# An LSTM step on one Trainium2 core: the scaled output gate is made on ScalarE instead of VectorE

## The chip, the cores and the metric

The kernel runs on one NeuronCore of a Trainium2 chip. TensorE (PE in the profile) multiplies matrices, VectorE (DVE) and ScalarE (ACT) work on tiles of up to 128 partitions, GpSimd (POOL) only clears some tiles at the start, and SyncE (SP) issues DMAs. Each engine takes its own instructions in order; engines wait for one another through semaphores. The metric is the time of one execution in microseconds (us), lower is better. Before the change the median of three runs is 1932.01 us (1931.52 to 1932.36).

## The reference

An LSTM with 512 hidden features runs over 512 time steps for a batch of 16, with float32 inputs, and its hidden states are added to the input:

```python
def step(carry, xw_t):
    prev_h, prev_c = carry
    a = xw_t + prev_h @ Wh
    i = sigmoid(a[:, :H]); f = sigmoid(a[:, H:2*H]); o = sigmoid(a[:, 2*H:3*H])
    g = tanh(a[:, 3*H:])
    next_c = f * prev_c + i * g
    next_h = o * tanh(next_c)
    return (next_h, next_c), next_h
# xW = x @ Wx + b for all steps;  output = x + hs
```

Step t+1 needs the h of step t, so 512 passes of the same chain stand one behind the other.

## The kernel before, in words

**The matmuls.** Every float32 factor is split into a high and a low float16 part, after scaling by a power of two. The weights stay in SBUF in both parts, with 256 columns to a matmul. One step is 128 matmuls of 32 columns of stationary data by 256 moving columns: 64 for the input part of the *next* step (`input_part`, L261), 32 with the low part of Wh (`recurrent_low`, L267) and 32 with the high part (`recurrent_high`, L273). The result lies in a PSUM tile `acc[par][n]`, where `par` is the parity of the step and `n` (0 or 1) one of two groups of 256 hidden features. ScalarE writes the bias into the tile ahead of the matmuls (`place_bias`, L202).

**The step behind the matmuls.** For each group n:

1. VectorE transposes the tile (`turn`, L439) and adds the two halves to the preactivations (`add_all` L448 for group 0; `add_three` L443 and `add_last` L451 for group 1).
2. ScalarE takes the tanh of three gates at once (`three_gates`, L216) and of the output gate alone (`last_gate`, L222). A sigmoid is made from a tanh of half the argument: sigmoid = (tanh + 1) / 2.
3. VectorE makes the two products of the cell (`gate_products`, L456) and the new cell (`new_cell`, L466); ScalarE takes the tanh of the cell (`tanh_of_cell`, L227).
4. The output gate is brought to (tanh + 1) times a scale of one number per partition, `scales[following][:, 1:2]` (`output_gate`, L461). It reads the tile of `last_gate`.
5. VectorE multiplies gate and cell tanh to the high half of h (`high_of_h`, L472), once more to the full h (`full_h`, L476), and subtracts to get the low half (`low_of_h`, L481).

**What the semaphores say.** TensorE waits for `h_high_ready` (counted by `high_of_h`) before the low-weight matmuls and for `h_ready` (counted by `low_of_h`) before the high-weight ones. It takes, in order: 16 low-weight matmuls on group 0 of h; 8 high-weight ones once the low half of h of group 0 is there; 8 low-weight ones once the high half of group 1 is there; then 8 high-weight ones once the low half of group 1 is there, which end `acc[par][0]` and let `turn(0)` start; 24 more end `acc[par][1]`; then come the 64 of the next step's input. `high_of_h(n)` waits for `h_parts_ready[n]`, which `output_gate(n)` and `tanh_of_cell(n)` count up by one each.

**The order** of all this is written out by hand, in the functions' calls at the end of each engine's step loop; no scheduler moves anything. The 512 steps come in 32 chunks of 16. Besides the above some steps carry work for the next chunk: input halves (ScalarE L183, VectorE L422), a search for the largest input (VectorE L517), one matmul L314 in step 8 of a chunk, and the scale of the next chunk in steps 9 to 13.

Of the kernel before, what the change touches and what calls it, by code (L numbers as in the profile page):

```python
# [5 lines left out]
ALU = mybir.AluOpType  # L6
ACT = mybir.ActivationFunctionType
# [8 lines left out]
NG = 2  # L16
CHUNK = 16
# [6 lines left out]
def lstm_kernel(nc, x, h0, wx, wh, bias, out):  # L24
# [7 lines left out]
    with ExitStack() as ctx:  # L32
        def sb(name, shape, dt):
            return ctx.enter_context(nc.sbuf_tensor(name, shape, dt))
# [4 lines left out]
        def sem(name):  # L39
            return ctx.enter_context(nc.semaphore(name))  # L40
# [29 lines left out]
        scales = [sb(f"scales{i}", [128, 4], F32) for i in range(2)]  # L70
# [10 lines left out]
        gates = [[sb(f"gates{p}{n}", [128, 5, 2 * B], F32) for n in range(NG)] for p in range(2)]  # L81
        products = [sb(f"products{n}", [128, 2, 2 * B], F32) for n in range(NG)]
        o_gate = [sb(f"o_gate{n}", [128, 2 * B], F32) for n in range(NG)]
# [38 lines left out]
        o_ready = sem("o_ready")  # L122
        products_ready = sem("products_ready")
        cell_ready = sem("cell_ready")
        h_parts_ready = [sem(f"h_parts_ready{n}") for n in range(NG)]
# [7 lines left out]
        @block.sync  # L133
        def _(sp):
            for c in range(C):
                sp.dma_start(w32["wx"][:, c, 0:Q], wx[:, c, 0:Q]).then_inc(w_loaded["wx"][c], 16)
            sp.dma_start(x_ring[0][:], x[:, 0:CHUNK, :]).then_inc(x_loaded[0], 16)
            for c in range(C):
                sp.dma_start(w32["wh"][:, c, 0:Q], wh[:, c, 0:Q]).then_inc(w_loaded["wh"][c], 16)
            sp.dma_start(x_ring[1][:], x[:, CHUNK:2 * CHUNK, :]).then_inc(x_loaded[1], 16)  # L140

            for first in range(0, T, QUARTER):
                chunk, at = divmod(first, CHUNK)
                half, slot = divmod(at, HALF)
                sp.wait_ge(out_ready, first + QUARTER)
                sp.dma_start(out[:, first:first + QUARTER, :], out_ring[half][:, slot:slot + QUARTER]).then_inc(out_free[half], 16)
                if chunk + 2 < CHUNKS:
                    sp.dma_start(x_ring[chunk % 2][:, at:at + QUARTER], x[:, first + 2 * CHUNK:first + 2 * CHUNK + QUARTER, :])\
                        .then_inc(x_loaded[chunk % 2], 16)
            for half in range(2):  # L150
                sp.wait_ge(out_free[half], 32 * CHUNKS + 1)
# [12 lines left out]
        @block.scalar  # L164
        def _(act):
            for c in range(C):
                act.dma_start(w32["wx"][:, c, Q:], wx[:, c, Q:]).then_inc(w_loaded["wx"][c], 16)
            act.dma_start(h0_feat[:], h0).then_inc(h0_loaded, 16)
            for c in range(C):
                act.dma_start(w32["wh"][:, c, Q:], wh[:, c, Q:]).then_inc(w_loaded["wh"][c], 16)  # L170
            act.dma_start(b_rows[:], bias).then_inc(b_loaded, 16)

            def high_of_w(k, n, c, done):
                act.activation(w_high[k][:, c, :, 0:64], w32[k][:, c, :, 0:64], ACT.Copy, scale=scale_bits[:, n:n + 1].bitcast(F32))
                act.activation(w_high[k][:, c, :, 64:GL], w32[k][:, c, :, 64:GL], ACT.Copy, scale=half_scale[:, n:n + 1])\
                    .then_inc(done, 1)

            act.wait_ge(wx_scale_ready, 1)
            for c in range(C):
                high_of_w("wx", 0, c, wx_high_done)  # L180
            def high_of_x(chunk, q):
                steps = slice(QUARTER * q, QUARTER * q + QUARTER)
                act.activation(x_halves[:, steps, :, 0, :], x_ring[chunk % 2][:, steps, :].rearrange("p t (c b) -> p t c b", b=B),  # L183
                               ACT.Copy, scale=scales[chunk % 2][:, 0:1]).then_inc(x_high_ready, 1)

            rescale = [act.alloc_register(f"rescale{p}") for p in range(2)]
            b_scale = [act.alloc_register(f"b_scale{p}") for p in range(2)]
            act.wait_ge(wh_scale_ready, 1)
            high_of_w("wh", 1, 0, wh_high_done)
            act.wait_ge(x_loaded[0], 16)  # L190
            act.wait_ge(x_scale_ready, 1)
            high_of_x(0, 0)
            high_of_w("wh", 1, 1, wh_high_done)
            high_of_x(0, 1)
            high_of_w("wh", 1, 2, wh_high_done)
            high_of_w("wh", 1, 3, wh_high_done)
            act.reg_load(rescale[0], inverses[0][0:1, 3:4])
            act.reg_load(b_scale[0], scales[0][0:1, 3:4].bitcast(I32))

            def place_bias(t):  # L200
                for n in range(NG):
                    act.activation(acc[t % 2][n][:, 0:GL], b_rows[:, n], ACT.Copy, scale=b_scale[t // CHUNK % 2])\  # L202
                        .then_inc(bias_placed, 1)

            act.wait_ge(b_ready, 1)
            act.wait_ge(acc_opened, 2 * NG)
            place_bias(0)

            for t in range(T):
                par = t % 2  # L210
                chunk, at = divmod(t, CHUNK)
                if t + 1 < T:
                    place_bias(t + 1)
                def three_gates(n):
                    act.wait_ge(preact_ready, NG * t + n + 1)
                    act.activation(gates[par][n][:, 1:4, :], preact[n][:, 0:6].rearrange("p (g c) b -> p g (c b)", c=2), ACT.Tanh,  # L216
                                   scale=rescale[chunk % 2]).then_inc(gates_ready, 1)

                def last_gate(n):
                    if n == 1:  # L220
                        act.wait_ge(o_preact_ready, t + 1)
                    act.activation(gates[par][n][:, 4, :], preact[n][:, 6:8].rearrange("p c b -> p (c b)"), ACT.Tanh,  # L222
                                   scale=rescale[chunk % 2]).then_inc(o_ready, 1)

                def tanh_of_cell(n):
                    act.wait_ge(cell_ready, NG * t + n + 1)
                    act.activation(cell_tanh[n][:], gates[1 - par][n][:, 0, :], ACT.Tanh, scale=0.5)\  # L227
                        .then_inc(h_parts_ready[n], 1)

                three_gates(0)  # L230
                last_gate(0)
                three_gates(1)
                tanh_of_cell(0)
                last_gate(1)
                tanh_of_cell(1)
                if at in (0, 1):
                    high_of_x(chunk, at + 2)
                if at in (13, 14) and chunk + 1 < CHUNKS:
                    if at == 13:
                        act.wait_ge(x_loaded[(chunk + 1) % 2], 16 + 16 * QUARTERS * ((chunk + 1) // 2))  # L240
                        act.wait_ge(x_scale_ready, chunk + 2)
                    high_of_x(chunk + 1, at - 13)
                    if at == 14:
                        act.reg_load(rescale[(chunk + 1) % 2], inverses[(chunk + 1) % 2][0:1, 3:4])
                        act.reg_load(b_scale[(chunk + 1) % 2], scales[(chunk + 1) % 2][0:1, 3:4].bitcast(I32))
# [71 lines left out]
        def _(dve):  # L317
# [112 lines left out]
            for t in range(T):  # L430
                par = t % 2
                chunk, at = divmod(t, CHUNK)
                later = (chunk + 1) % 2
                following = (t + 1) // CHUNK % 2
                nth = [NG * t + n + 1 for n in range(NG)]
# [14 lines left out]
                def add_last(n):  # L450
                    dve.tensor_tensor(preact[n][:, 6:8], turned[n][:, 6:8, 0, :], turned[n][:, 6:8, 1, :], ALU.add)\  # L451
                        .then_inc(o_preact_ready, 1)
# [3 lines left out]
                    dve.scalar_tensor_tensor(products[n][:], gates[par][n][:, 2:4, :], 1.0, gates[par][n][:, 0:2, :],  # L456
                                             ALU.add, ALU.mult).then_inc(products_ready, 1)

                def output_gate(n):
                    dve.wait_ge(o_ready, nth[n])  # L460
                    dve.tensor_scalar(o_gate[n][:], gates[par][n][:, 4, :], 1.0, scales[following][:, 1:2], ALU.add, ALU.mult)\  # L461
                        .then_inc(h_parts_ready[n], 1)

                def new_cell(n):
                    dve.wait_ge(products_ready, nth[n])
                    dve.scalar_tensor_tensor(gates[1 - par][n][:, 0, :], products[n][:, 0, :], 0.5, products[n][:, 1, :],  # L466
                                             ALU.mult, ALU.add).then_inc(cell_ready, 1)
# [19 lines left out]
                gate_products(0)  # L487
                add_three(1)
                new_cell(0)
                output_gate(0)  # L490
                add_last(1)
                gate_products(1)
                high_of_h(0)
                new_cell(1)
                full_h(0)
                output_gate(1)
                low_of_h(0)
                high_of_h(1)
                full_h(1)
# [81 lines left out]
```

## Time and profile before

| what | value |
|---|---|
| median of the runs | 1932.01 us |
| profiled execution, its own time | 1936.5 us |
| its span, first to last instruction | 1934.7 us |
| granted TensorE clock, share of full speed | 0.998 |
| PE busy | 1877.5 us, 97% of the span |
| DVE busy | 1816.8 us, 94% |
| ACT busy | 990.9 us, 51% |
| output gate on DVE (L461) | 1024 instructions, mean 234 ns |
| cell tanh on ACT (L227) | 1024 instructions, mean 221 ns |

A busy share is the share of time in which at least one instruction of an engine is in flight. Instructions of one engine overlap at their edges, so the busy times of single instructions add up to more than the time they take in a row; the distance between two starts tells how long one holds the engine. The rows of a timeline have the start in us, the duration in us, the engine, the line of the kernel, the operation and its tiles, and in brackets how long the engine was idle before it and what it waited for.

### The profile page before, as it was taken

The page shows a single profiled execution, that of the slowest core. Times are in us where ns is not written, and L with a number is a line of the kernel's source. Part 1 is how long each engine was busy: PE and PEld are TensorE (multiplying, and loading weights), DVE is VectorE, ACT ScalarE, POOL GpSimd, SP SyncE. Part 2 cuts the span into 40 slices and gives each one's busy share as a digit, 9 for nine tenths or more (in the row PEclk, how much of TensorE's full clock was granted, in tenths as well). Part 3 has the DMA queues.
Part 4 walks back from the last instruction along what each step waited for, and adds up shares of the span by engine and source line. Part 5 has one row for each costly group of instructions (what it writes and reads, how often), then busy time and mean ns, then how long its engine had stood idle before and what let it go on. Part 6 is the DMA issues. An engine that isn't in the chain of part 4 may idle for free.

```text
span 1934.7 us, 145599 instructions
## 1 busy us (share of the span) xinstructions
PE 1877.5 (97%) x65588; PEld 1630.8 (84%) x65588; DVE 1816.8 (94%) x9739; ACT 990.9 (51%) x4241; POOL 2.6 (0%) x14
## 2 busy tenths in 40 slices
PE   1999999999999999999999999999999999999998
PEld 0888888888888888888888888888888888888887
DVE  8899999999999999999999999999999999999998
ACT  4455555555555555555555555555545555555554
POOL 0000000000000000000000000000000000000000
PEclk9999999999999999999999999999999999999999
DMA  5000000000000000000000000000000000000000
GB/s 201 15 27 22 21 26 21 22 21 27 21 21 27 21 21 24 24 22 21 27 21 21 26 22 21 24 24 22 21 26 21 21 27 22 21 21 27 18 13 15
DMA packets 39216, 51.56 MB, mean 27 GB/s; under 512 B 4416, under 2 KB 36160, under 8 KB 38592
## 3 DMA queue, kind: packets, MB, share of 16 engines
q1 hardware_dynamic: 37152, 37.77, 6.0%
q8 instruction: 512, 8.39, 1.8%
q10 hardware_dynamic: 1440, 4.49, 0.6%
q14 instruction: 112, 0.92, 0.2%
HBM read 25.46 MB, written 16.78 MB: 22 GB/s over the span
## 4 chain that ended last, share of the span: by engine, by line
PE 91%; DVE 6%; ACT 1%; DMA 1%; issue 1%; ACTq 0%; DVEq 0%
PE acc L261 44%; PE acc L267 23%; PE acc L273 23%; DVE turned L439 1%; DMA wh<-in_wh 1%; ACT x_halves L183 1%; DVE products L456 1%; DVE o_gate L461 0%; DVE preact L448 0%; DVE h_halves L481 0%; ACT acc L202 0%; DVE wx_low L341 0%; DVE h_halves L472 0%; DVE wh_low L341 0%; DVE gates L466 0%
## 5 line engine op out<-in xcount | busy, mean ns | idle before, releaser
L261 PE MATMUL acc<-wx_high,x_halves 128*32 128x256 f16 x16384 | 938.6, 273 | 6.4 <-ACT acc L202 2.6
L261 PE MATMUL acc<-wx_low,x_halves 128*32 128x256 f16 x16384 | 940.4, 273 | 3.0 <-issue 2.4
L267 PE MATMUL acc<-wh_low,h_halves 128*32 128x256 f16 x16384 | 726.9, 274 | 4.3 <-DVE wh_low L341 4.0
L273 PE MATMUL acc<-wh_high,h_halves 128*32 128x256 f16 x16384 | 728.8, 275 | 0.0
L216 ACT ACTIVATE gates<-preact 128x96 f32<-128x96 f32 x1024 | 289.3, 283 | 774.7 <-DVE preact L448 599.7
L439 DVE STREAM_TRANSPOSE turned<-acc 128x256 f32<-128x256 f32 x1024 | 456.6, 446 | 69.7 <-PE acc L273 63.1
L261 PEld LDWEIGHTS acc<-wx_high,x_halves 128*32 128x32 f16 x16384 | 461.9, 97 | 26.7 <-ACT acc L202 11.1
L261 PEld LDWEIGHTS acc<-wx_low,x_halves 128*32 128x32 f16 x16384 | 465.0, 97 | 20.3 <-issue 10.3
L267 PEld LDWEIGHTS acc<-wh_low,h_halves 128*32 128x32 f16 x16384 | 398.8, 96 | 92.5 <-DVE h_halves L472 71.9
L273 PEld LDWEIGHTS acc<-wh_high,h_halves 128*32 128x32 f16 x16384 | 365.4, 96 | 113.7
L202 ACT ACTIVATE acc<-b_rows 128x256 f32<-128x256 f32 x1024 | 345.4, 369 | 0.8 <-issue 0.3
L227 ACT ACTIVATE cell_tanh<-gates 128x32 f32<-128x32 f32 x1024 | 226.5, 221 | 113.3 <-DVE gates L466 113.3
L461 DVE TENSOR_SCALAR o_gate<-gates,scales 128x32 f32<-128x32 f32 x1024 | 239.3, 234 | 0.0
L456 DVE SCALAR_TENSOR_TENSOR products<-gates 128x64 f32<-128x64 f32 x1024 | 230.7, 225 | 1.9
L222 ACT ACTIVATE gates<-preact 128x32 f32<-128x32 f32 x1024 | 226.2, 221 | 0.0
L481 DVE TENSOR_TENSOR h_halves<-h_feat,h_halves 128x32 f16<-128x32 f32 x1024 | 191.5, 187 | 17.8
L472 DVE TENSOR_TENSOR h_halves<-o_gate,cell_tanh 128x32 f16<-128x32 f32 x1024 | 192.7, 188 | 0.0
L466 DVE SCALAR_TENSOR_TENSOR gates<-products 128x32 f32<-128x32 f32 x1024 | 192.4, 188 | 0.0
L476 DVE TENSOR_TENSOR h_feat<-o_gate,cell_tanh 128x32 f32<-128x32 f32 x1024 | 188.2, 184 | 0.0
L448 DVE TENSOR_TENSOR preact<-turned 128x128 f32<-128x128 f32 x512 | 149.3, 292 | 17.6
L505 DVE SCALAR_TENSOR_TENSOR out_ring<-h_feat,inverses,x_ring 128x64 f32<-128x64 f32 x512 | 142.1, 278 | 0.0
L443 DVE TENSOR_TENSOR preact<-turned 128x96 f32<-128x96 f32 x512 | 128.9, 252 | 0.0
(62 smaller groups left out, 388.5 us busy)
## 6 DMA issues: line engine op xcount, KB each, us to landing
out<-out_ring SPq DMA_DIRECT2D x128, 128.0 KB, 1.7
x_ring<-in_x SPq DMA_DIRECT2D x120, 128.0 KB, 2.2
wx<-in_wx ACTq DMA_DIRECT2D x4, 512.0 KB, 8.1
wx<-in_wx SPq DMA_DIRECT2D x4, 512.0 KB, 8.1
wh<-in_wh SPq DMA_DIRECT2D x4, 512.0 KB, 16.7
wh<-in_wh ACTq DMA_DIRECT2D x4, 512.0 KB, 17.2
x_ring<-in_x SPq DMA_DIRECT2D x2, 512.0 KB, 16.7
b_rows<-in_b ACTq DMA_DIRECT2D x1, 256.0 KB, 21.4
```

The source lines that it names most:

```text
L202: act.activation(acc[t % 2][n][:, 0:GL], b_rows[:, n], ACT.Copy, scale=b_scale[t // CHUNK % 2])\
L216: act.activation(gates[par][n][:, 1:4, :], preact[n][:, 0:6].rearrange("p (g c) b -> p g (c b)", c=2), ACT.Tanh, scale=rescale[chunk % 2]) ...
L222: act.activation(gates[par][n][:, 4, :], preact[n][:, 6:8].rearrange("p c b -> p (c b)"), ACT.Tanh, scale=rescale[chunk % 2]).then_inc(o_r ...
L227: act.activation(cell_tanh[n][:], gates[1 - par][n][:, 0, :], ACT.Tanh, scale=0.5)\
L261: pe.matmul(acc[par][n][32 * j:32 * j + 32, 0:GL], x_halves[:, slot, c], w[:, c, n * Q + j], start=False, stop=False, skip_group_check=True)
L267: pe.matmul(acc[par][n][32 * j:32 * j + 32, 0:GL], h_halves[1 - par][:, c, 0:2], w_low["wh"][:, c, n * Q + j], start=False, stop=False, sk ...
L273: last = pe.matmul(acc[par][n][32 * j:32 * j + 32, 0:GL], h_halves[1 - par][:, c, 1:3], w_high["wh"][:, c, n * Q + j], start=False, stop=c ...
L439: dve.transpose(turned[n][:].rearrange("p g s b -> p (g s b)"), acc[par][n][:, 0:GL]).then_inc(turned_ready, 1)
L456: dve.scalar_tensor_tensor(products[n][:], gates[par][n][:, 2:4, :], 1.0, gates[par][n][:, 0:2, :], ALU.add, ALU.mult).then_inc(products_r ...
L461: dve.tensor_scalar(o_gate[n][:], gates[par][n][:, 4, :], 1.0, scales[following][:, 1:2], ALU.add, ALU.mult)\
L466: dve.scalar_tensor_tensor(gates[1 - par][n][:, 0, :], products[n][:, 0, :], 0.5, products[n][:, 1, :], ALU.mult, ALU.add).then_inc(cell_r ...
L472: dve.tensor_tensor(h_halves[par][:, 2 * n:2 * n + 2, 1, :], og, ct, ALU.mult).then_inc(h_high_ready, 1)
```

## The change

`output_gate(n)` leaves VectorE. ScalarE gets an activation with the function Identity, with the scale and also the bias taken from the same 128x1 column of `scales`: scale * tanh + scale = (tanh + 1) * scale. It stands right behind `last_gate(n)` and waits for that instruction's own semaphore. TensorE's, GpSimd's and SyncE's instructions stay as they were. The built program still has one table load on ScalarE, ahead of its first activation.

```diff
+                following = (t + 1) // CHUNK % 2        # in ScalarE's step loop
...
+                def output_gate(n):
+                    act.wait_ge(o_ready, NG * t + n + 1)
+                    act.activation(o_gate[n][:], gates[par][n][:, 4, :], ACT.Identity, bias=scales[following][:, 1:2],
+                                   scale=scales[following][:, 1:2]).then_inc(h_parts_ready[n], 1)
...
                 three_gates(0)
                 last_gate(0)
+                output_gate(0)
                 three_gates(1)
                 tanh_of_cell(0)
                 last_gate(1)
+                output_gate(1)
                 tanh_of_cell(1)
...
-                def output_gate(n):                     # in VectorE's step loop
-                    dve.wait_ge(o_ready, nth[n])
-                    dve.tensor_scalar(o_gate[n][:], gates[par][n][:, 4, :], 1.0, scales[following][:, 1:2], ALU.add, ALU.mult)\
-                        .then_inc(h_parts_ready[n], 1)
...
                 gate_products(0)
                 add_three(1)
                 new_cell(0)
-                output_gate(0)
                 add_last(1)
                 gate_products(1)
                 high_of_h(0)
                 new_cell(1)
                 full_h(0)
-                output_gate(1)
                 low_of_h(0)
                 high_of_h(1)
                 full_h(1)
```

ScalarE, one step, before (the digit behind `gates` is first the parity of the step, then the group; the digit behind the other tiles is the group):

```order
L216 ACTIVATE gates10<-preact0 128x96 [waits preact_ready]
L222 ACTIVATE gates10<-preact0 128x32
L216 ACTIVATE gates11<-preact1 128x96 [waits preact_ready]
L227 ACTIVATE cell_tanh0<-gates00 128x32 [waits cell_ready]
L222 ACTIVATE gates11<-preact1 128x32 [waits o_preact_ready]
L227 ACTIVATE cell_tanh1<-gates01 128x32 [waits cell_ready]
```

The same step of ScalarE now:

```order
L217 ACTIVATE gates10<-preact0 128x96 [waits preact_ready]
L223 ACTIVATE gates10<-preact0 128x32
L228 ACTIVATE o_gate0<-gates10,scales0 128x32 [waits o_ready]
L217 ACTIVATE gates11<-preact1 128x96 [waits preact_ready]
L233 ACTIVATE cell_tanh0<-gates00 128x32 [waits cell_ready]
L223 ACTIVATE gates11<-preact1 128x32 [waits o_preact_ready]
L228 ACTIVATE o_gate1<-gates11,scales0 128x32 [waits o_ready]
L233 ACTIVATE cell_tanh1<-gates01 128x32 [waits cell_ready]
```

The two L228 rows are new: one stands between the output gate's tanh of group 0 and the three gates of group 1, the other between the output gate's tanh of group 1 and the tanh of group 1's cell.

VectorE, the middle of one step, before:

```order
L466 SCALAR_TENSOR_TENSOR gates10<-products0 128x32 [waits products_ready]
L461 TENSOR_SCALAR o_gate0<-gates00,scales0 128x32 [waits o_ready]
L451 TENSOR_TENSOR preact1<-turned1 128x32
L456 SCALAR_TENSOR_TENSOR products1<-gates01 128x64 [waits gates_ready]
L472 TENSOR_TENSOR h_halves0<-o_gate0,cell_tanh0 128x2x16 [waits h_parts_ready0]
L466 SCALAR_TENSOR_TENSOR gates11<-products1 128x32 [waits products_ready]
L476 TENSOR_TENSOR h_feat0<-o_gate0,cell_tanh0 128x32
L461 TENSOR_SCALAR o_gate1<-gates01,scales0 128x32 [waits o_ready]
L481 TENSOR_TENSOR h_halves0<-h_feat0,h_halves0 128x2x16 [waits h_feat_ready]
L472 TENSOR_TENSOR h_halves0<-o_gate1,cell_tanh1 128x2x16 [waits h_parts_ready1]
```

And now:

```order
L469 SCALAR_TENSOR_TENSOR gates10<-products0 128x32 [waits products_ready]
L459 TENSOR_TENSOR preact1<-turned1 128x32
L464 SCALAR_TENSOR_TENSOR products1<-gates01 128x64 [waits gates_ready]
L475 TENSOR_TENSOR h_halves0<-o_gate0,cell_tanh0 128x2x16 [waits h_parts_ready0]
L469 SCALAR_TENSOR_TENSOR gates11<-products1 128x32 [waits products_ready]
L479 TENSOR_TENSOR h_feat0<-o_gate0,cell_tanh0 128x32
L484 TENSOR_TENSOR h_halves0<-h_feat0,h_halves0 128x2x16 [waits h_feat_ready]
L475 TENSOR_TENSOR h_halves0<-o_gate1,cell_tanh1 128x2x16 [waits h_parts_ready1]
```

The two TENSOR_SCALAR rows are gone and the rest stands as it did.

## Rows read from the trace of the kernel before

**Rows 1.** The page: busy time by engine, and the chain that ended last, by engine.

```profile
PE 1877.5 (97%) x65588; PEld 1630.8 (84%) x65588; DVE 1816.8 (94%) x9739; ACT 990.9 (51%) x4241; POOL 2.6 (0%) x14
...
PE 91%; DVE 6%; ACT 1%; DMA 1%; issue 1%; ACTq 0%; DVEq 0%
```

**Rows 2.** Timeline of TensorE in an ordinary step: start us, duration us, instruction.

```profile
1042.80 0.62 PE L267 MATMUL acc<-wh_low,h_halves 128*32 128x256 f16 x16
...
1043.27 0.40 PE L273 MATMUL acc<-wh_high,h_halves 128*32 128x256 f16 x8
...
1043.73 0.62 PE L273 MATMUL acc<-wh_high,h_halves 128*32 128x256 f16 x16
```

**Rows 3.** Timeline of VectorE in the same step.

```profile
1040.55 0.45 DVE L439 STREAM_TRANSPOSE turned<-acc 128x256 f32<-128x256 f32 x1 [0.17 <-PE acc L273]
...
1041.98 0.18 DVE L466 SCALAR_TENSOR_TENSOR gates<-products 128x32 f32<-128x32 f32 x1
1042.09 0.23 DVE L461 TENSOR_SCALAR o_gate<-gates,scales 128x32 f32<-128x32 f32 x1
...
1042.23 0.18 DVE L451 TENSOR_TENSOR preact<-turned 128x32 f32<-128x32 f32 x1
...
1042.41 0.23 DVE L456 SCALAR_TENSOR_TENSOR products<-gates 128x64 f32<-128x64 f32 x1
...
1042.67 0.19 DVE L466 SCALAR_TENSOR_TENSOR gates<-products 128x32 f32<-128x32 f32 x1
1042.79 0.18 DVE L476 TENSOR_TENSOR h_feat<-o_gate,cell_tanh 128x32 f32<-128x32 f32 x1
...
1042.89 0.23 DVE L461 TENSOR_SCALAR o_gate<-gates,scales 128x32 f32<-128x32 f32 x1
...
1043.03 0.18 DVE L481 TENSOR_TENSOR h_halves<-h_feat,h_halves 128x32 f16<-128x32 f32 x1
1043.16 0.19 DVE L472 TENSOR_TENSOR h_halves<-o_gate,cell_tanh 128x32 f16<-128x32 f32 x1
...
1043.49 0.19 DVE L481 TENSOR_TENSOR h_halves<-h_feat,h_halves 128x32 f16<-128x32 f32 x1
...
1044.19 0.45 DVE L439 STREAM_TRANSPOSE turned<-acc 128x256 f32<-128x256 f32 x1 [0.23 <-PE acc L273]
```

**Rows 4.** Timeline of ScalarE in the same step.

```profile
1041.55 0.21 ACT L222 ACTIVATE gates<-preact 128x32 f32<-128x32 f32 x1
...
1042.10 0.28 ACT L216 ACTIVATE gates<-preact 128x96 f32<-128x96 f32 x1 [0.34 <-DVE preact L443]
...
1042.29 0.21 ACT L227 ACTIVATE cell_tanh<-gates 128x32 f32<-128x32 f32 x1
...
1042.45 0.23 ACT L222 ACTIVATE gates<-preact 128x32 f32<-128x32 f32 x1
...
1042.90 0.23 ACT L227 ACTIVATE cell_tanh<-gates 128x32 f32<-128x32 f32 x1 [0.22 <-DVE gates L466]
```

**Rows 5.** ScalarE's durations, min/median/max in ns of L222 and L183; mean of L175.

```profile
L222 ACT ACTIVATE gates<-preact x1024: 212/222/233, 54.4 to 1931.1; 128x32 f32<-128x32 f32 x171
...
L183 ACT ACTIVATE x_halves<-x_ring,scales x128: 491/494/510, 35.2 to 1880.7; 128x256 f16<-128x256 f32 x128
...
L175 ACT ACTIVATE wx_high<-wx,half_scale 128x1536 f16<-128x1536 f32 x4 | 6.2, 1560 | 0.0
```

**Rows 6.** Timelines of a chunk's step 8, then its step 14.

```profile
1024.65 0.62 PE L267 MATMUL acc<-wh_low,h_halves 128*32 128x256 f16 x16
...
1025.20 0.19 DVE L481 TENSOR_TENSOR h_halves<-h_feat,h_halves 128x32 f16<-128x32 f32 x1
...
1025.53 0.61 PE L273 MATMUL acc<-wh_high,h_halves 128*32 128x256 f16 x16
...
1047.20 0.19 DVE L481 TENSOR_TENSOR h_halves<-h_feat,h_halves 128x32 f16<-128x32 f32 x1
...
1047.52 0.61 PE L273 MATMUL acc<-wh_high,h_halves 128*32 128x256 f16 x16
```

## The prediction

> **What bounds the kernel now.** I read the page first. TensorE is in flight for 97% of the span and makes up 91% of the chain that ended last, with VectorE at 94% and ScalarE at 51% [rows 1]. Read alone this says that TensorE sets the time, and that moving work from a full VectorE to a half idle ScalarE can only help. So I read one step as a timeline, engine by engine, and asked of each start what ended last before it.
>
> A step takes 3.64 us, from one turn(0) to the next: 1040.55 to 1044.19, and both times VectorE stood idle until TensorE released it, 0.17 and 0.23 us [rows 3]. TensorE does not run without a gap either. The 32 matmuls ahead of the one batch that ends acc[par][0] take 0.88 us, 1024.65 to 1025.53, in a step where it has nothing to wait for [rows 6]; that is 0.44 for sixteen and 0.22 for eight. In the ordinary step the same 32 take 1042.80 to 1043.73, 0.93 us [rows 2]. The 0.05 us are waits for halves of h. So the step is a loop through all three engines: turn(0), gates, cell, tanh of the cell, halves of h, matmuls, turn(0). TensorE's busy share hides this, because some matmul is in flight nearly always.
>
> Next, where the loop is tight. The low half of h of group 1 is written from 1043.49 for 0.19, to 1043.68 [rows 3], and TensorE goes on with the high-weight matmuls at 1043.73 [rows 2]: 0.05 is the hand-over from VectorE to TensorE. Those matmuls end acc[par][0], and turn(0) follows at 1044.19. So this wait decides. Back from there: low_of_h(1) follows full_h(1), that follows high_of_h(1) at 1043.16, and that waits for the tanh of group 1's cell, 1042.90 + 0.23 = 1043.13 [rows 3, 4]. That tanh waits for new_cell(1), 1042.67 + 0.19 = 1042.86, and ScalarE had been idle for 0.22 before it. Between VectorE and ScalarE a hand-over takes 0.03 to 0.04.
>
> **The change part by part.**
>
> *Taken from VectorE:* two instructions of 0.23 a step. By the distances of starts each holds VectorE for 0.14: 1042.09 to 1042.23, and 1042.89 to 1043.03 [rows 3]. That would be 1024 x 0.14 = 143 us if VectorE were the bound. It is not, at either place. Behind the first stands gate_products(1) at 1042.41, which waits for ScalarE's three gates of group 1, 1042.10 + 0.28 = 1042.38 [rows 4]; only add_last(1) between them comes earlier, at 1042.09. Behind the second, low_of_h(0) can move from 1043.03 to 1043.00 (full_h(0) at 1042.79 + 0.18, and a hand-over), and TensorE's second piece from 1043.27 to 1043.24, but its piece at 1043.73 waits for group 1's low half, which did not move: high_of_h(1) at 1043.16 waits for ScalarE. Gain in the loop: nothing. What hides it is ScalarE's chain of tanhs, on the very engine that gets the work.
>
> *The price of the new instruction.* No Identity with scale and bias from memory stands in the trace. Nearest rows: an activation on 128x32 whose scale is a register or a constant takes 212 ns, or 229 to 233 where it had to wait for its semaphore (the two ends of the first of [rows 5]). L183 and L175 read their scale from a 128x1 column: 494 ns for 256 elements and 1560 for 1536 [rows 5], that is 0.833 ns an element, so 494 - 224 x 0.833 = 307 ns for 32 elements, 95 more than without the column. The new one has two such columns. If the second costs as much as the first: 307 + 95 = 402, and 17 more because it waits for the tanh just before it: 419 ns. If the second were free: 324 ns. I take 419: scale and bias are two operands of the instruction, even where both name the same column; 324 and 419 are kept for the range.
>
> The Trainium skill (ScalarE: Activation LUTs, What ACT_TABLE_LOAD costs) gives 186 ns + 0.833 ns an element with immediates, about 93 ns more for each pointer operand, and an overlap of about 93 ns between activations in a row. The rows agree on the first pointer (95) and on the overlap below; no row has a second one. By that page the instruction takes about 399 ns, an estimate, and the sum below would be some 20 ns a step less, about 1954 us.
>
> *Group 0.* last_gate(0) ends at 1041.55 + 0.21 = 1041.76 [rows 4]. Hand-over 0.035, start 1041.795, duration 0.419. An activation that need not wait starts 0.09 before the end of the one ahead (the three gates end at 1042.38, the cell tanh starts at 1042.29). So three_gates(1) starts at 1041.795 + 0.419 - 0.09 = 1042.12, against 1042.10 now. The idle 0.34 in front of it is just filled. As it need not wait any more it also takes 0.017 less, and ends at 1042.39 against 1042.38: at most 0.01 comes out, and I count 0.005.
>
> *Group 1.* The cell tanh of group 0 starts at 1042.29. last_gate(1) no longer waits for add_last(1), which is done by 1042.27, and starts 0.12 behind it (0.21 - 0.09), at 1042.41 instead of 1042.45, ending 1042.62. Hand-over: 1042.66. The output gate ends at 1043.08. The cell tanh of group 1 starts 0.09 before, at 1042.99 in place of 1042.90, takes 0.213 since it need not wait, and ends at 1043.20. Now it ends at 1043.13. It ends 0.07 later, of which nothing is hidden: high_of_h(1), full_h(1), low_of_h(1) and TensorE's piece at 1043.73 follow it one by one. Group 0's 0.005 is within the rounding of this. So the step grows by 0.07, from 3.64 to 3.71. Behind the cell tanh on ScalarE stand the two place_bias; the matmuls that need them come after turn(0), more than a microsecond later, so they cost nothing.
>
> *Which steps.* In step 8 of a chunk TensorE is late because of its extra matmul: the low half is there at 1025.20 + 0.19 + 0.05 = 1025.44, and TensorE comes at 1025.53 [rows 6], 0.09 of cover. In step 14 it is late because the bias was placed late, 1047.44 against 1047.52 [rows 6], 0.08. Both swallow 0.07. These are 2 x 31 steps (the last chunk has neither); 450 are left. VectorE's extra work of other steps moves with the loop and ends no later against turn(0).
>
> *The sum:* 450 x 0.07 = 31.5 us. The profiled execution would go from 1936.5 to 1968; against the median, 4.5 us lower, 1932.0 + 31.5 = 1963.5 us.
>
> **The rivals.**
>
> *The ScalarE hole holds it.* If the second column is read beside the first, the output gate takes 324 ns, the cell tanh of group 1 could start 0.095 earlier than above, at 1042.90, and it starts there as now. Then nothing on the loop moves: 1932, within 2 us. For it: both operands are the same column. Against it: the first column alone costs 95 ns on this engine. In the same way it would hold if ScalarE let an instruction start earlier behind one that only reads columns at first; no row shows more than 0.10 of overlap. Chance 0.12.
>
> *VectorE was the bound after all, faster.* TensorE's first gap, 1043.24 to 1043.27, goes since low_of_h(0) comes earlier, and the extra searches and halves leave VectorE sooner. For it: VectorE's 94%. Its price: the gap is 0.03 a step, but past it TensorE has only 0.02 left to gain up to 1043.73, so 512 x 0.02 = 10 us, 1922. It decides only if group 1's low half also comes earlier, and that hangs on the cell tanh, whose release at 1042.86 VectorE does not bring forward. Chance 0.03.
>
> *Slower by more.* A result that ScalarE reads back right behind its own write may be handed over later than between two engines: VectorE to TensorE takes 0.05 in the rows. With 0.055 in both groups in place of 0.035, group 0's start moves 0.02 and group 1's 0.02 more: 0.11 a step, 450 x 0.11 = 49.5, 1981.5; at this size steps 8 and 14 give up 0.02 to 0.03 as well. Chance 0.10, as the upper part of slower.
>
> **How the numbers follow.** The forecast with its small deviations has 0.75 (0.05 to 0.09 a step, 1954 to 1973), slower by more 0.10, no change 0.12, faster 0.03. A measurement of this kernel tells about 0.2%, 4 us, from no change. All but the last two are slower: 0.85; same 0.12; faster 0.03. The range goes from 0.03 a step (a second column that is half hidden, 1946) to 1981; it leaves out the no-change case.
>
> **What would show it.** Right: in the new trace the output gate on ScalarE takes 0.40 to 0.42 us, ScalarE has no idle time before the cell tanh of group 1 (0.22 in [rows 4]), VectorE's new_cell(1) is done well before that tanh starts, and a step is 3.71. Wrong: an output gate of about 0.32, or a cell tanh of group 1 that still starts 0.04 behind new_cell(1)'s end; then the step is still 3.64. If the output gate takes 0.42 and the time is unchanged, my reading of the wait at 1043.73 is wrong.

## The result and the profile after

The change makes the kernel slower: 1956.41 us (median of four, 1956.2 to 1957.2) against 1932.18 for the kernel before on the same occasion. The ratio is 1.0126, with a 95% interval of 1.0115 to 1.0138, so 24 us. Forecast were 1963.5 us, a range of 1946 to 1981 and a chance of 0.85 for slower. The profiled execution took 1956.5 us (span 1954.6, granted TensorE clock 1.0).

The page first, the row that answers to [rows 1], and the chain by engine:

```profile
PE 1901.7 (97%) x65588; PEld 1582.2 (81%) x65588; DVE 1742.1 (89%) x8715; ACT 1272.2 (65%) x5265; POOL 2.6 (0%) x14
...
PE 90%; DVE 5%; ACT 3%; DMA 1%; issue 1%; ACTq 0%; DVEq 0%
```

VectorE lost 75 us of busy time and ScalarE gained 281. TensorE still shows 97%, and still it is not what sets the step (the run with eight matmuls less, below, shows it).

ScalarE in one step, whose turn(0) starts at 1040.60. It answers to [rows 4], where turn(0) starts at 1040.55:

```profile
1041.59 0.21 ACT L223 ACTIVATE gates<-preact 128x32 f32<-128x32 f32 x1
...
1041.84 0.41 ACT L228 ACTIVATE o_gate<-gates,scales 128x32 f32<-128x32 f32 x1
...
1042.16 0.27 ACT L217 ACTIVATE gates<-preact 128x96 f32<-128x96 f32 x1
...
1042.34 0.21 ACT L233 ACTIVATE cell_tanh<-gates 128x32 f32<-128x32 f32 x1
...
1042.46 0.21 ACT L223 ACTIVATE gates<-preact 128x32 f32<-128x32 f32 x1
...
1042.70 0.41 ACT L228 ACTIVATE o_gate<-gates,scales 128x32 f32<-128x32 f32 x1
...
1043.02 0.21 ACT L233 ACTIVATE cell_tanh<-gates 128x32 f32<-128x32 f32 x1
```

None of these rows has an idle time in brackets any more; in [rows 4] two of them had, 0.34 and 0.22. Read from the end: the cell tanh of group 1 starts at 1043.02, 0.09 before the output gate ahead of it ends (1043.11). It does not wait for its cell, which VectorE finished at 1042.72 + 0.19 = 1042.91, as VectorE's rows of the same step show (compare [rows 3]):

```profile
1042.72 0.19 DVE L469 SCALAR_TENSOR_TENSOR gates<-products 128x32 f32<-128x32 f32 x1
...
1043.27 0.19 DVE L475 TENSOR_TENSOR h_halves<-o_gate,cell_tanh 128x32 f16<-128x32 f32 x1
...
1043.60 0.19 DVE L484 TENSOR_TENSOR h_halves<-h_feat,h_halves 128x32 f16<-128x32 f32 x1
...
1044.30 0.45 DVE L447 STREAM_TRANSPOSE turned<-acc 128x256 f32<-128x256 f32 x1
```

And TensorE in that step, against [rows 2]:

```profile
1042.85 0.62 PE L275 MATMUL acc<-wh_low,h_halves 128*32 128x256 f16 x16
...
1043.30 0.40 PE L281 MATMUL acc<-wh_high,h_halves 128*32 128x256 f16 x8
...
1043.84 0.62 PE L281 MATMUL acc<-wh_high,h_halves 128*32 128x256 f16 x16
```

Counted from turn(0), before and after: cell tanh of group 1 ends at 2.58 and 2.63; high_of_h(1) starts at 2.61 and 2.67; low_of_h(1) at 2.94 and 3.00; TensorE's high-weight matmuls at 3.18 and 3.24; next turn(0) at 3.64 and 3.70. One delay of 0.06 (0.05 at its first row, by rounding) is handed from row to row. TensorE's start of the step (2.25 in both) did not move, and its second piece came 0.02 earlier (2.72, now 2.70), which is lost again at the third.

The new instruction's own time, minimum, median, maximum in ns:

```profile
L228 ACT ACTIVATE o_gate<-gates,scales x1024: 412/413/416, 54.7 to 1951.2; 128x32 f32<-128x32 f32 x171
```

By the starts of all turn(0)s the median step went from 3.642 to 3.702, except for step 8 of a chunk (3.717 in both) and step 14 (3.776, now 3.770). 450 x 0.060 = 27.0 us. The medians of the runs differ by 24.2. Where the other 3 us may come from is taken up with the change's second run, below.

### The profile page after: what moved, and what is told of

The parts are those of the page before. It is cut to its first block, busy times and chain, and to the rows that moved or that the text cites. A ratio compares the mean times of both kernels' runs of the same rounds, so it can differ in the third digit from the quotient of the medians.

```text
span 1954.6 us, 145599 instructions
## 1 busy us (share of the span) xinstructions
PE 1901.7 (97%) x65588; PEld 1582.2 (81%) x65588; DVE 1742.1 (89%) x8715; ACT 1272.2 (65%) x5265; POOL 2.6 (0%) x14
## 3 DMA queue, kind: packets, MB, share of 16 engines
q8 instruction: 512, 8.39, 1.7%
## 4 chain that ended last, share of the span: by engine, by line
PE 90%; DVE 5%; ACT 3%; DMA 1%; issue 1%; ACTq 0%; DVEq 0%
PE acc L269 43%; PE acc L281 24%; PE acc L275 23%; DMA wh<-in_wh 1%; ACT x_halves L183 1%; ACT gates L217 1%; DVE turned L447 1%; ACT o_gate L228 1%; DVE h_halves L484 1%; DVE preact L456 0%; DVE h_halves L475 0%; ACT acc L202 0%; DVE h_feat L479 0%; DVE products L464 0%; DVE wx_low L349 0%
## 5 line engine op out<-in xcount | busy, mean ns | idle before, releaser
L269 PE MATMUL acc<-wx_low,x_halves 128*32 128x256 f16 x16384 | 929.2, 273 | 0.0
L275 PE MATMUL acc<-wh_low,h_halves 128*32 128x256 f16 x16384 | 719.5, 274 | 4.0 <-DVE wh_low L349 4.0
L281 PEld LDWEIGHTS acc<-wh_high,h_halves 128*32 128x32 f16 x16384 | 349.9, 96 | 153.8 <-DVE h_halves L484 91.5
L275 PEld LDWEIGHTS acc<-wh_low,h_halves 128*32 128x32 f16 x16384 | 353.3, 96 | 134.5 <-DVE h_halves L475 81.9
L269 PEld LDWEIGHTS acc<-wx_high,x_halves 128*32 128x32 f16 x16384 | 438.7, 97 | 24.0 <-ACT acc L202 11.6
L269 PEld LDWEIGHTS acc<-wx_low,x_halves 128*32 128x32 f16 x16384 | 438.7, 97 | 9.4
L228 ACT ACTIVATE o_gate<-gates,scales 128x32 f32<-128x32 f32 x1024 | 423.4, 413 | 34.1
L233 ACT ACTIVATE cell_tanh<-gates 128x32 f32<-128x32 f32 x1024 | 217.8, 213 | 0.0
L223 ACT ACTIVATE gates<-preact 128x32 f32<-128x32 f32 x1024 | 217.8, 213 | 0.0
```

The costliest lines, as they stand in the source:

```text
L228: act.activation(o_gate[n][:], gates[par][n][:, 4, :], ACT.Identity, bias=scales[following][:, 1:2], scale=scales[following][:, 1:2]).then ...
L269: pe.matmul(acc[par][n][32 * j:32 * j + 32, 0:GL], x_halves[:, slot, c], w[:, c, n * Q + j], start=False, stop=False, skip_group_check=True)
L275: pe.matmul(acc[par][n][32 * j:32 * j + 32, 0:GL], h_halves[1 - par][:, c, 0:2], w_low["wh"][:, c, n * Q + j], start=False, stop=False, sk ...
L281: last = pe.matmul(acc[par][n][32 * j:32 * j + 32, 0:GL], h_halves[1 - par][:, c, 1:3], w_high["wh"][:, c, n * Q + j], start=False, stop=c ...
```

## The experiments

**Group 0 alone on ScalarE.** Group 1's output gate is back on VectorE:

```diff
                 last_gate(1)
-                output_gate(1)          # ScalarE
...
                 full_h(0)
+                output_gate(1)          # VectorE
                 low_of_h(0)
```

> Only group 0's output gate is on ScalarE; group 1's is on VectorE as before. Theory (the loop goes through the cell tanh of group 1, and ScalarE has a hole of 0.34 us ahead of group 0's place): a step stays 3.64 us within 0.005, 1932 us, within 2 us. Rival A (each output gate on ScalarE costs its half of the loss): +12 us, 1944. Rival B (VectorE's freed 0.14 us a step is worth something): faster, by up to 512 x 0.14 = 72 us, 1860; 1925 if only a tenth of it counts.

Measured: 1948.87 us against 1950.32 for the kernel before with it, ratio 0.9992 (0.9978 to 1.0006): no change, and neither half of the loss nor a gain through VectorE. The median step of its profile is 3.65. The kernel before was not profiled on this occasion; its step was 3.64 on the first, and the run without any output gate, below, has 3.65 as well. ScalarE in one step:

```profile
1043.65 0.41 ACT L228 ACTIVATE o_gate<-gates,scales 128x32 f32<-128x32 f32 x1
1043.97 0.27 ACT L217 ACTIVATE gates<-preact 128x96 f32<-128x96 f32 x1
...
1044.26 0.21 ACT L223 ACTIVATE gates<-preact 128x32 f32<-128x32 f32 x1
1044.76 0.23 ACT L233 ACTIVATE cell_tanh<-gates 128x32 f32<-128x32 f32 x1 [0.28 <-DVE gates L473]
```

The same 0.41 us, at a place with room, costs nothing that can be measured. And the cell tanh of group 1 waits for its cell again, 0.28 us now, since last_gate(1) in front of it no longer waits for add_last(1). The expected absolute time was wrong by 17 us, for the kernel before as well; more of that below.

**Group 1 alone on ScalarE.** The mirror image: ScalarE's output_gate(0) goes, VectorE's stands behind new_cell(0) as before the change.

```diff
                 last_gate(0)
-                output_gate(0)          # ScalarE
...
                 new_cell(0)
+                output_gate(0)          # VectorE
                 add_last(1)
```

> Only group 1's output gate is on ScalarE; group 0's is on VectorE as before. Theory: worse than both together, because VectorE's output_gate(0) holds back add_last(1) again and so last_gate(1), which the new instruction waits for: last_gate(1) from 1042.45 to 1042.68 as before, output gate to 1042.715 + 0.413 = 1043.13, cell tanh from 1043.04 to 1043.25 against 1043.13 before: 0.12 us a step, 450 x 0.12 + 62 x 0.035 = 56 us, 1988. Rival A (each gate its half): +12, 1944. Rival (the whole loss belongs to group 1, no more and no less): +24, 1956.

Measured: 1986.49 us against 1950.32 for the kernel before with it, ratio 1.0184 (1.0164 to 1.0205), so 36 us slower and not the 56 that were expected. The absolute time came out as the sum said (1988), because the sum started from 1932 and the kernel before took 1950 here; the change once more, below, takes this up. The step is 3.76, as expected, and both rivals (1944, 1956) are out. It is also 25 to 30 us more than the two occasions on which the change with both on ScalarE was timed. VectorE and ScalarE in one step:

```profile
1042.98 0.23 DVE L468 TENSOR_SCALAR o_gate<-gates,scales 128x32 f32<-128x32 f32 x1
...
1043.12 0.18 DVE L458 TENSOR_TENSOR preact<-turned 128x32 f32<-128x32 f32 x1
...
1043.18 0.21 ACT L233 ACTIVATE cell_tanh<-gates 128x32 f32<-128x32 f32 x1
...
1043.34 0.23 ACT L223 ACTIVATE gates<-preact 128x32 f32<-128x32 f32 x1
...
1043.60 0.41 ACT L228 ACTIVATE o_gate<-gates,scales 128x32 f32<-128x32 f32 x1
...
1043.92 0.21 ACT L233 ACTIVATE cell_tanh<-gates 128x32 f32<-128x32 f32 x1
```

VectorE's output gate of group 0 stands before add_last(1), so that last_gate(1) starts 0.16 behind the cell tanh at 1043.18 instead of 0.12 behind it, and takes 0.02 longer because it waits. Both delays go straight into the loop through the new instruction. So the halves of the change don't add: 0 for group 0, 0.118 us a step for group 1, 0.060 for both. The move of group 0 makes room for group 1's new instruction, and in these rows that is all it does.

**One column instead of two.** The scale comes from a register that is loaded once a chunk, the bias from the column; both gates on ScalarE, the result the same.

```diff
                     act.activation(o_gate[n][:], gates[par][n][:, 4, :], ACT.Identity, bias=scales[following][:, 1:2],
-                                   scale=scales[following][:, 1:2]).then_inc(h_parts_ready[n], 1)
+                                   scale=h_scale[following]).then_inc(h_parts_ready[n], 1)
```

> Both output gates on ScalarE as in the change, but the scale comes from a register and only the bias from a 128x1 column; the register is loaded once a chunk. Theory (the second column's 95 ns are what does not fit into ScalarE's hole): the instruction takes about 0.32 us, the cell tanh of group 1 can start at 1042.66 + 0.32 - 0.09 = 1042.89, just when the cell releases it; a step is 3.64 again, 1932 us, within 3. Rival (any instruction between last_gate(1) and the cell tanh costs, by its wait on its own engine): at least half of the 24 us stays, 1944 or more. Rival (the column is free, the time lies in Identity): the instruction takes 0.41 as before and nothing changes, 1956.

Measured: 1948.64 us against 1950.32, ratio 0.9995 (0.9981 to 1.0009). The duration of its output gate, minimum, median, maximum in ns:

```profile
L230 ACT ACTIVATE o_gate<-gates,scales x1024: 321/322/324, 54.6 to 1943.0; 128x32 f32<-128x32 f32 x171
```

And the end of one of its steps:

```profile
1043.69 0.32 ACT L230 ACTIVATE o_gate<-gates,scales 128x32 f32<-128x32 f32 x1
1043.71 0.19 DVE L472 SCALAR_TENSOR_TENSOR gates<-products 128x32 f32<-128x32 f32 x1
1043.94 0.23 ACT L235 ACTIVATE cell_tanh<-gates 128x32 f32<-128x32 f32 x1
```

413 - 322 = 91 ns for the second column, and without it the loss is gone, to within the interval; the median step is 3.65 in place of 3.70. The cell tanh takes 0.23 again: it waits for its cell (1043.90 and the hand-over) and no longer for the output gate. Both the operand's price and the size of the hole can be read from this. With group 0's gate on ScalarE, the hole in front of the cell tanh of group 1 is 0.28 us, as the run with group 0 alone showed. An instruction put there takes up a hand-over of 0.03 and its duration, less the 0.09 by which the next one overlaps it: 0.03 + 0.32 - 0.09 = 0.26 fits, 0.03 + 0.41 - 0.09 = 0.35 does not. What sticks out is 0.07, less 0.02 because the tanh no longer waits: 0.05, an estimate, against 0.06 measured. For group 1 alone the hole is 0.22, and the same sum gives 0.11, against 0.118.

**No output gate on either engine.** The products of h read the tanh of the output gate itself, which leaves out the scaling and the + 1.

```diff
-                    og, ct = (k[n][:].rearrange("p (c b) -> p c b", b=B) for k in (o_gate, cell_tanh))
-                    dve.wait_ge(h_parts_ready[n], 2 * (t + 1))
+                    og, ct = (k.rearrange("p (c b) -> p c b", b=B) for k in (gates[par][n][:, 4, :], cell_tanh[n][:]))
+                    dve.wait_ge(h_parts_ready[n], t + 1)
...
                 new_cell(0)
-                output_gate(0)
...
                 full_h(0)
-                output_gate(1)
```

> The scaled output gate is left out on both engines: the products of h read the tanh of the output gate itself, so h is wrong and unscaled. Everything else as before the change. It shows what VectorE's relief alone is worth. Theory: nothing, a step stays 3.64 us, 1932 us, within 2. Rival (VectorE was the bound): 2 x 0.14 us a step, 512 x 0.28 = 143 us, 1789; with TensorE's own limit of 128 matmuls at 0.0273 = 3.49 us a step it would end near 1855. Rival (a small gain through the earlier low half of group 0): 0.02 a step, 1922.

Measured: 1950.15 us against 1950.32, ratio 0.9997 (0.9984 to 1.0010). Taking 1024 instructions off an engine that is busy for 94% of the span, and giving them to nobody, brings nothing; the median step is 3.65. The end of a step:

```profile
1044.09 0.23 ACT L227 ACTIVATE cell_tanh<-gates 128x32 f32<-128x32 f32 x1 [0.28 <-DVE gates L461]
...
1044.19 0.19 DVE L476 TENSOR_TENSOR h_halves<-h_feat,h_halves 128x32 f16<-128x32 f32 x1
...
1044.35 0.19 DVE L467 TENSOR_TENSOR h_halves<-gates,cell_tanh 128x32 f16<-128x32 f32 x1
```

high_of_h(1) starts at 1044.35, 0.03 behind the end of the tanh (1044.32), and 0.16 behind low_of_h(0), which would have held VectorE for some 0.11 only. It waits for ScalarE. VectorE's relief is filled by waiting.

**The change once more, with its own runs of the kernel before.** In the four runs above the kernel before took 1942 to 1956 us (median 1950) where it had taken 1932, and group 1 alone came out as worked out only in its absolute time. So I asked what the slower ones had.

> The change itself once more, on a chip whose runs of the kernel before are timed with it. In the four experiments so far the kernel before took 1950 us where it had taken 1932, and the traces of the kernels near it show TensorE waiting for 'issue' some 80 to 120 times, while group 1 alone, with a step of 3.76, shows hardly any. Theory C (these gaps come only where TensorE runs almost without a wait; a step of 3.70 is free of them): 1956 to 1957 again on any chip, so the loss is 24 us where the kernel before takes 1932 and 6 us where it takes 1950. Rival (the chips of the later runs are slower by a share, whatever the kernel): 1956 x 1950 / 1932 = 1975.

Measured: 1961.33 us against 1940.98, ratio 1.0102 (1.0083 to 1.0122), a loss of 20 us. TensorE's weight loads of the input part waiting for "issue", in total us, times and longest. The first profile of the kernel before:

```profile
PEld acc L261 <- issue: 13.2, 41, 0.6
```

Group 0 alone:

```profile
PEld acc L268 <- issue: 27.1, 79, 0.6
```

No output gate:

```profile
PEld acc L261 <- issue: 40.3, 116, 0.6
```

This run of the change (its first profile has no such row):

```profile
PEld acc L269 <- issue: 17.8, 48, 0.6
```

Group 1 alone:

```profile
PEld acc L268 <- issue: 2.5, 9, 0.5
```

"Issue" is a wait for nothing that the profile shows. One such wait of the kernel before, in a step of 4.02 us (1770.67 to 1774.69):

```profile
1770.67 0.45 DVE L439 STREAM_TRANSPOSE turned<-acc 128x256 f32<-128x256 f32 x1
...
1772.39 0.10 PEld L261 LDWEIGHTS acc<-wx_low,x_halves 128*32 128x32 f16 x3 [0.62 <-issue]
1772.39 0.29 PE L261 MATMUL acc<-wx_low,x_halves 128*32 128x256 f16 x3 [0.34 <-issue]
...
1774.69 0.45 DVE L439 STREAM_TRANSPOSE turned<-acc 128x256 f32<-128x256 f32 x1 [0.36 <-PE acc L273]
```

By the starts of turn(0), apart from the first step, 44 steps of the first profile of the kernel before are more than 0.02 us over the median of their place in the chunk, 7.9 us in all; in that of the change there are none. Here the change has 48, 8.6 us in all. So the half of my expectation that the change is free of them was wrong: it had none on the first occasion and has some here, where the kernel before was not profiled beside it. The forecast of 1956 to 1957 on any chip missed with it. The rival's 1975 was worked out for a kernel before of 1950; with the 1941 of this occasion a share of the whole makes 1965, and four runs of 1958 to 1964 hardly tell that from a constant. Group 1 alone tells: where the kernel before took 1950 it came in at 1986, and a share would have turned its 1988 into some 2006.

For the two profiled executions of the first occasion the sum closes nearly: 27.0 us of longer steps less 7.9 us of late ones is 19.1, and they took 1936.5 and 1956.5, 20.0 apart. The 24.2 us between the medians would want about 3 us of late steps in the kernel before. No profile of such a run was kept, so this part is argued and not shown.

**Eight matmuls less a step.** The low part of Wx is left out for one of four blocks of the input.

```diff
                 for c in range(C):
-                    for w in (w_high["wx"], w_low["wx"]):
+                    for w in (w_high["wx"], w_low["wx"])[:2 if c < C - 1 else 1]:
```

> The kernel before, but a step has 120 matmuls in place of 128: the low part of Wx is left out for one of four blocks of the input, so the preactivations are a little off. TensorE gets 8 x 0.0273 = 0.22 us of spare time a step, all in the input part, which nothing in the loop waits for. Theory C (the kernel before loses its issue gaps because TensorE has no spare time): the step stays 3.64 us by the loop and the gaps vanish or are hidden, 1926 to 1930 us on any chip: 3 us less than the kernel before where it takes 1932, 20 less where it takes 1950. Steps 8 and 14 of a chunk lose TensorE's lateness too, up to 6 us more. Rival (the gaps come at times of their own, wherever TensorE stands): the time stays that of the kernel before, less the 6 us. Rival (TensorE's matmuls are the bound): 0.22 a step less, 112 us, 1820 to 1840.

Measured: 1924.77 us, five runs within 2.1 us, against 1940.98 (1934.6 to 1944.4); ratio 0.9918 (0.9903 to 0.9934). Busy times on its page:

```profile
PE 1817.6 (94%) x61492; PEld 1497.4 (78%) x61492; DVE 1814.1 (94%) x9739; ACT 990.7 (51%) x4241; POOL 2.6 (0%) x14
```

Its chain that ended last, by engine, which was 91% PE before, and two of its waits:

```profile
DVE 74%; PE 21%; ACT 2%; issue 2%; DMA 1%; ACTq 0%; DVEq 0%
...
PEld acc L267 <- DVE h_halves L472: 183.8, 478, 0.4
...
PEld acc L261 <- issue: 0.9, 2, 0.7
```

Two readings at once. The step stays 3.64: 0.22 us less work for TensorE a step takes nothing off the ordinary step, it only turns into waiting for h (183.8 us in total). And with spare time in TensorE the issue waits are 2 in place of 41 or more, and the runs lie closer together. Of the 16 us that it gained, 4.3 come from steps 8 and 14 of each chunk, whose medians went from 3.717 to 3.642 and from 3.776 to 3.712; the time is 1 us under the range expected. This run has 6% fewer instructions on TensorE as well as more spare time. Group 1 alone has all of the instructions and 0.12 us more spare time a step, and stopped 9 times, so fewer instructions are not needed for that.

**A better order.** The rows say that the loop starts with turn(0), the sum of group 0, its gates. Group 0's sum takes 0.29 us for all gates; three gates alone take 0.25.

```diff
-                add_all(0)
+                add_three(0)
+                add_last(0)
                 turn(1)
```

with last_gate(0) on ScalarE waiting for add_last(0). Once with both output gates on VectorE:

> The kernel before with group 0's sum split like group 1's (three gates first, then the last), output gates on VectorE. Theory of the loop: the three gates of group 0 are ready 0.04 us earlier, turn(1) starts 0.06 later, and gate_products(0) behind turn(1) starts 0.015 earlier; a step is 3.63, 7 us less by the loop. Theory C: TensorE then waits less for h and has more issue gaps, so the 7 us are given back wholly or partly: between the kernel before and 7 us less. Rival (turn(1) is what counts): 0.06 a step more, +27 us.

Measured: 1935.98 us against 1940.98, ratio 0.9979 (0.9964 to 0.9993). The step is 3.622, so 0.020 less, a little more than the 0.015 expected; 450 x 0.020 = 9 us, of which 5 arrive. The rival, 27 us more, is out. And once with group 0's output gate on ScalarE on top:

> The same split with group 0's output gate on ScalarE, group 1's on VectorE: the best order that the rows give. By the loop 0.015 us a step less, like the split alone, since group 0's output gate lies in ScalarE's hole: 7 us less than before. Theory C: as for the split alone, given back wholly or partly in issue gaps. Rival (ScalarE's hole is too short here): the three gates of group 1 start later and the time is that of before or more.

Measured: 1937.39 us, ratio 0.9977 (0.9964 to 0.9989), the same as the split alone. Both beat the kernel before by 0.2%, and the change by 1.2 to 1.3% on the same occasion; they can't be told from each other.

## Why the prediction was right

*The bound.* Right. The wait at 1043.73 decided, and the chain in front of it is group 1's cell tanh. Eight matmuls less left the step at 3.64.

*Nothing for VectorE's relief.* Right: ratio 0.9997 with both instructions gone. The small move of group 0's low half came (2.72 to 2.70 from turn(0)) and was swallowed at the next wait, as the prediction had it.

*The price of the instruction.* 413 ns measured, 419 predicted. The second column cost 91 ns, the first had given 95 [rows 5]; taking the same price twice was right, and the rival in which the second is free fell. The estimate from the Trainium skill (ScalarE: Activation LUTs, What ACT_TABLE_LOAD costs) was 399 ns. The trace agrees with its price for an operand to 2 ns (93 there, 91 here); with the 17 ns that a waiting activation takes more in the rows it makes 416.

*Group 0.* Right: hidden. Alone it costs nothing that can be measured.

*Group 1.* The mechanism was right and the size 0.01 us too high: 0.070 predicted, 0.060 measured. Of the 0.010, 0.006 are the duration and the rest lies in the hand-over on ScalarE itself, 0.03 where I had 0.035, and in the shift of group 0. On 450 steps that makes 27.0 in place of 31.5.

*Which steps.* Right: step 8 stayed at 3.717, step 14 even went from 3.776 to 3.770. 450 steps bear the loss.

*The part that was missing.* 27.0 by the loop, 24.2 measured. The kernel before carries issue waits, and the change had none in its first profile; with 0.06 us more spare time a step for TensorE this is what the runs with still more of it (group 1 alone, eight matmuls less) lead one to expect. The prediction took the difference between the profiled execution and the median (4.5 us) as a constant and did not look at the steps of 4.0 us from which it comes, though the row "PEld acc L261 <- issue" was in the trace. How large this part is differs from occasion to occasion: the change lost 24 us at first, and 20 when run again. The direction held each time. The forecast of 1963.5 was 7 us too high, 4.5 by the size of the step and nearly 3 by this part: the two errors add up, and neither hid the other.

## What to carry to other kernels

A half idle engine is no free engine: ask for the length of each hole between the instructions of the chain, not for the busy share, and price the moved instruction with its operands. Here the same instruction, which takes up 0.35 us of such a hole, cost nothing measurable in one of 0.34 us, 0.060 us a step in one of 0.28 and 0.118 in one of 0.22. In the one of 0.28, an operand of 91 ns decided between a loss of 20 to 24 us and none. And two halves of an edit need not add up, since one of them may be what feeds the other.

## What the runs showed of the hardware

- An activation on 128x32 takes 213 ns without an operand in memory, 322 with one column and a wait, 413 with two and a wait. A tensor_scalar on VectorE with a constant and one column takes 234, and holds its engine for 0.14.
- An instruction that waits for the write of the one before it on ScalarE starts 0.03 us after its end (1042.67 to 1042.70), no later than one that waits for VectorE.
- TensorE, with 256 instructions (128 matmuls and as many weight loads) in 3.64 us and about 0.15 us of them spare (an estimate, from the 0.11 us between the starts of four matmuls and the next four), stops now and then for up to 0.6 us, a third of a us in the mean, with nothing to wait for that the profile shows: 41 to 116 times in the profiles of six kernels with a step of 3.62 to 3.65. The kernel before, among them, had medians of 1932, 1950 and 1941 us on three occasions, while the change's two were 1956 and 1961. The last two occasions were on two different chips, so the occasion and the chip can't be told apart here. With 0.22 us more spare a step it stopped twice, and five runs lay within 2.1 us.
- The page's queue for instructions (q8) moves 8.39 MB in 512 packets in each of these six kernels, about one packet a step. The stops go with these packets. Over the ten traces TensorE's weight loads have 556 stops of over 0.15 us put down to "issue" in the recurrent steps behind the first 80 us, and each of them ends between 1.19 and 1.64 us after such a packet has ended; of moments picked at random 12% lie so. The packet in question had ended 3.87 us behind the one before it (median), against 3.71 for all packets. So a stop lasts until shortly after a late packet of instructions. This is read from the records of the packets; no run changed them, and why some come late stays open.
